# Two-layer block on one core: another order of product, squares, silu, low parts and fourth powers in the first stage

## The chip, the core and the metric

The kernel runs on one NeuronCore of a Trainium2 chip. It is one launch that holds the whole network: TensorE for the matrix products, VectorE, ScalarE and GpSimd beside it, SyncE for the loads and stores. The metric is the device time in microseconds. Lower is better.

## The reference

The input is 2048 tokens of width 256 (8 x 256 x 256, float32). Four parts follow each other, each with a residual sum and a layer norm:

```python
x = _layernorm(x + _L0_attn_ref(x, ...))   # 16 heads of 16, rope, layernorm of q and k, causal scores ** 4
x = _layernorm(x + _L0_ffn_ref(x, ...))    # silu(x @ gate.T) * (x @ up.T), hidden width 1024, then down
x = _layernorm(x + _L1_attn_ref(x, ...))   # 32 heads of 8, softmax with a relative bias
x = _layernorm(x + _L1_ffn_ref(x, ...))    # 8 experts, top 2, and a shared expert
```

The change lies in the first two of these. Of the first attention, for each batch of 256 tokens:

```python
q = layernorm(rope(q), ln_scale, ln_bias)
k = layernorm(rope(k), ln_scale, ln_bias)
a = tril(einsum(q, k) ** 4)
out = einsum(a / sum(a), v)
```

## The kernel before

Every float32 product is made of three matrix products of a high and a low part (`product3`, lines 443 to 445), so what enters a product is first written as a high part by ScalarE (`..._hi`) and then, as the difference to it, a low part by VectorE (`..._lo`).

The first stage takes the first attention and the first feed-forward net together. It has 8 iterations `i` of one batch of 256 tokens, and each has 8 slots `p`, one for each pair of heads. All engines run a program of their own, in an order that is written out by hand in the functions `slot` and `narrow_slot` (and in `dense` for what fills a slot), and they wait for each other at semaphores alone. An engine works strictly in the order in which its program stands: a wait holds back all that is written behind it.

What a slot holds, by engine, with the lines that a profile shows:

- TensorE: `scores` of pair p (729, 730), `gate_up(m)` of one hidden tile of 128 of the feed-forward net of an earlier batch (12 products `ps<-WU` of 128x256), in odd slots `mix` (747, the product with v of four heads), then a part of the attention of this or the next batch (`heads`, 676, turns q and k; `v`; `qk`; `x_turn`; `c_turn`; `ct_turn`, 697; `project`), and last `down(m - 1)` (6 products `ps<-WU`).
- ScalarE: `square` of the scores (1398), `hidden_hi(m - 1)` (1417), in even slots `quartic` of the odd pair p - 1 (1381), `silu(m)` (1410), and others, among them `centred_squares(i + 1)` (1352), `deviation(i + 1)` (1357), `head_hi_parts(i + 1)` (1368) and `x_hi` (1309).
- VectorE: in odd slots `quartic` of the even pair p - 1 (1937), `hidden_lo(m - 1)` (1955), `product(m)` (1949, up part times silu), and the chain that makes q and k of the next batch: `rope_half` (1881 to 1884), `rotated` (1889 adds, 1890 sums over each head), `centre` (1895), `variance` (1900), `normalised` (1907, 1908), `times_scale` (1914), `plus_bias` (1918), `lo_parts` (1928). Further `x1_added` and `x1_statistics` (1825 to 1833) and `x1_norm` (1841), the norm behind the feed-forward net, `context_lo` (1804) and `x_lo` (1776).
- GpSimd: `masks` (2511), the lower triangle of each squared pair; in iteration 2 also the low parts of the weights (2463).

Iterations 0 and 1 have no feed-forward tiles yet and run `narrow_slot`; iterations 2 to 7 run `slot`. The feed-forward net lags by `LAG1 = 2` batches, so m = 8 * (i - 2) + p - 1. After iteration 7 stand 16 more tiles of it, and then the second attention and the experts, which the change does not touch.

The waits that tie the engines in a slot:

```python
pe.wait_ge(prod_ready[1], m)              # gate_up(m): the bank of gates must be read by product(m - 1)
pe.wait_ge(hid_ready[1], m + 1)           # down(m): hidden_lo(m)
pe.wait_ge(ffn_step, 3 * b - 2)           # down(m) of a batch's first tile: x1_added of the batch before
act.wait_ge(quartic_even, H0 // 4 * i + p // 2)   # square(i, p), even p: quartic(i, p - 2)
act.wait_ge(in_step, IN_STEPS * b + 8)    # centred_squares(b): centre(b)
act.wait_ge(in_step, IN_STEPS * b + 13)   # head_hi_parts(b): plus_bias(b)
dve.wait_ge(hid_hi[1], m + 1)             # hidden_lo(m): hidden_hi(m)
dve.wait_ge(masked, H0 // 2 * i + p + 1)  # quartic(i, p): masks(i, p)
pe.wait_ge(ct_ready[0], i)                # project and heads of the next batch: context_lo(i - 1)
```

Of the kernel before, what the change touches and what calls it, by code (L numbers as in the profile page):

```python
# [47 lines left out]
LAG1 = 2  # L48
# [39 lines left out]
def program(nc, x, rope, ln, aw0, wu1, aw2, rel, wu3, router, sel, out):  # L88
    with ExitStack() as ctx:
# [1213 lines left out]
        def _(act):  # L1303
# [37 lines left out]
            def first_layer():  # L1341
# [6 lines left out]
                n = iterations[0]  # L1348

                def centred_squares(b):  # L1350
                    act.wait_ge(in_step, IN_STEPS * b + 8)
                    act.square(SQ, CEN).then_inc(cen_squared, 1)
# [52 lines left out]
                def silu(m):  # L1405

                    act.wait_ge(gate_ready[1], m + 1)
                    if m >= 2:
                        act.wait_ge(prod_ready[1], m - 1)
                    act.activation(sg[:, m % 2, :], ps[:, gate_bank(m), 0:S], ACT.Silu).then_inc(silu_ready[1], 1)  # L1410
# [74 lines left out]
                def slot(i, p):  # L1485

                    m = H0 // 2 * (i - LAG1) + p - 1
                    square(i, p)
                    if p == 2 and i < n - 1:
                        centred_squares(i + 1)  # L1490
                    if m >= 1:
                        hidden_hi(m - 1)
                    if p % 2 == 0 and (p or i):
                        quartic(i, p - 1, not i)
                    if m >= 0:
                        silu(m)
                    dense(i, p)
                    if i == LAG1 and p < TILES1 - 1:
                        raw_hi(p + 1)
                    if p == 3 and i < n - 1:  # L1500
                        deviation(i + 1)
# [232 lines left out]
        def _(dve):  # L1734
# [109 lines left out]
            def first_layer():  # L1844
# [22 lines left out]
                n = iterations[0]  # L1867
# [18 lines left out]
                def rotated(b):  # L1886

                    dve.wait_ge(in_step, IN_STEPS * b + 6)
                    step(rope_added, b + 1, dve.tensor_tensor(ROT, ROT, ROT2, ALU.add))
                    step(in_step, IN_STEPS * b + 7, dve.tensor_reduce(hsum, rh, AX_X, ALU.add))  # L1890

                def centre(b):
# [64 lines left out]

                def narrow_slot(i, p):

                    if p % 2:  # L1960
                        quartic(i, p - 1, not i)
                    if p == 1:
                        rotated(i + 1)
                    if p == 2:
                        centre(i + 1)
                    if p == 3:
                        times_scale(i + 1)
                        if i:
                            for c in range(2):
                                context(0, i - 1, c, D0)  # L1970
                        variance(i + 1)
                    if p == 4:
                        x_lo(0, i + 2)
                        normalised(i + 1)
                    if p == 5:
                        if i:
                            context_lo(0, i - 1)
                        plus_bias(i + 1)
                    if p == 6:
                        lo_parts(i + 1, 0)  # L1980
                        lo_parts(i + 1, 1)
                        if i:
                            dve.wait_ge(y_ready[0], i)
                            add(0, i - 1, 2, xr_a, (B_Y[0],))
                            statistics(0, i - 1, 2, xr_a)
                    if p == 7:
                        if i:
                            norm(0, i - 1, 2, xr_a, X1[(i - 1) % 2])
                        dve.wait_ge(split_ready[0], 8 * (i + 2))
                        rope_half(i + 2, 0)  # L1990
                        if not i:
                            rope_half(i + 2, 1)

                def slot(i, p):

                    m = H0 // 2 * (i - LAG1) + p - 1
                    left = n - 1 - i
                    if p % 2:
                        quartic(i, p - 1, not i)
                    if m >= 1:  # L2000
                        hidden_lo(m - 1)
                    if p == 1 and left:
                        rotated(i + 1)
                    if p == 2 and i > LAG1:
# [13 lines left out]
                    if p == 0:  # L2018
                        x1_lo(i - LAG1)
                        if left:  # L2020
                            rope_half(i + 1, 1)
                    if p == 1 and left:
                        centre(i + 1)
                    if p == 2 and left:
                        variance(i + 1)
# [6 lines left out]
                    if p == 4:  # L2032
                        if left:
                            plus_bias(i + 1)
                        if i > LAG1:
                            x1_norm(i - LAG1 - 1)
                    if p == 5 and i:
                        context_lo(0, i - 1)
                    if p == 5 and left:
                        lo_parts(i + 1, 0)  # L2040
                    if p == 6 and i:
                        dve.wait_ge(y_ready[0], i)
                        add(0, i - 1, 2, xr_a, (B_Y[0],))
                        statistics(0, i - 1, 2, xr_a)
# [7 lines left out]
                diagonal()  # L2052
                rope_half(0, 1)
                rotated(0)
                centre(0)
                times_scale(0)
                variance(0)
# [680 lines left out]
```

## Time and profile before

| | |
|---|---|
| device time, median of 3 runs | 912.49 us (912.26 to 913.99) |
| the profiled execution | 913.56 us, its span 911.8 us |
| mean granted clock of TensorE | 0.974 of full speed |
| busy in the span | PE 90%, PEld 76%, DVE 72%, ACT 64%, POOL 48% |
| iterations 0 and 1 | about 30 to 80.5 us from the span's start |
| iteration 2 | about 80.5 to 124 us |
| iterations 3 to 7 | about 124 to 316 us, 39.1 us each, the last 35.4 us |

In a profile PE is TensorE, DVE VectorE, ACT ScalarE, POOL GpSimd. In a row of the timeline the first number is the start, the second the time taken, both in us; the bracket gives how long the engine stood idle before it and which engine and line released it. Consecutive matmuls overlap, so their times sum to more than the clock shows. A row that joins several instructions says xN.

### The profile page before, as it was taken

The numbers are of one execution on the slowest core, as the hardware profiler recorded it, in microseconds if no ns is written. First come the engines' busy times: TensorE is split into PE (matmuls) and PEld (weight loads), VectorE is DVE, ScalarE is ACT, GpSimd is POOL, SyncE is SP. The second block draws the span as 40 slices with busy tenths as digits, with TensorE's granted clock in tenths as the row PEclk, the third lists the DMA queues.
The fourth block names the chain that finished last, engine by engine and source line by source line (L and its number), as shares of the span: only waits on it lengthen the run. The fifth ranks groups of instructions, "written<-read, shape, count | busy, mean of one in ns | idle before, by whom it ended". The sixth has DMA issues, their size and how long they took to land.

```text
span 911.8 us, 20877 instructions
## 1 busy us (share of the span) xinstructions
PE 819.4 (90%) x7136; PEld 692.3 (76%) x7136; DVE 653.8 (72%) x2050; ACT 581.4 (64%) x1230; POOL 435.2 (48%) x733
## 2 busy tenths in 40 slices
PE   3877889999989999789999999999988999899994
PEld 2555778888878899666777777776766888899984
DVE  6978779788885555778798888889785553365447
ACT  2787958677685533678777777778765233366646
POOL 0346632332343220566766767666754366244423
PEclk9899999999999999899999999999999899899998
DMA  7201220210000010101020221101013112244434
GB/s 209 69 3 46 72 82 13 82 47 1 25 24 25 25 47 12 52 22 29 22 61 14 60 59 27 52 22 41 22 56 122 40 65 82 82 123 120 127 140 184
DMA packets 54761, 54.86 MB, mean 60 GB/s; under 512 B 17953, under 2 KB 48929, under 8 KB 54658
## 3 DMA queue, kind: packets, MB, share of 16 engines
q1 hardware_dynamic: 51250, 44.18, 16.7%
q0 software_dynamic: 3408, 9.34, 2.9%
q8 instruction: 60, 0.98, 0.4%
q14 instruction: 43, 0.35, 0.1%
HBM read 32.85 MB, written 20.65 MB: 59 GB/s over the span
## 4 chain that ended last, share of the span: by engine, by line
PE 60%; DVE 14%; ACT 11%; issue 7%; POOL 5%; DMA 3%; SPq 0%; ACTq 0%; DVEq 0%; POOLq 0%
PE ps L443 11%; PE ps L978 10%; PE ps L445 10%; PE ps L444 10%; PE ps L992 7%; POOL xs L2630 3%; ACT G L1566 2%; PE ps L963 2%; PE ps L676 2%; ACT G L1564 2%; PE ps L747 2%; PE ps L689 1%; DVE G L2127 1%; DVE ring L1937 1%; PE ps L1192 1%
## 5 line engine op out<-in xcount | busy, mean ns | idle before, releaser
L2511 POOL TENSOR_SCALAR_AFFINE_SELECT G<-G 128x256 f32<-128x256 f32 x128 | 77.2, 626 | 145.1 <-ACT G L1398 144.9
L1564 ACT ACTIVATE G<-ps 128x512 f32<-128x512 f32 x184 | 102.8, 602 | 49.8 <-PE ps L978 49.8
L443 PE MATMUL ps<-WU 128*128 128x256 f32 x384 | 117.1, 305 | 17.1 <-DVE wu_rows L1949 6.9
L2566 POOL TENSOR_SCALAR G<-G,small 128x256 f32<-128x256 f32 x214 | 99.4, 480 | 55.2 <-DVE small L2127 54.4
L2127 DVE CUSTOM_DVE_ANT_0 G<-ps,nb 128x256 f32<-128x256 f32 x296 | 108.3, 420 | 10.6 <-PE ps L963 9.7
L444 PE MATMUL ps<-WU 128*128 128x256 f32 x384 | 108.6, 283 | 0.0
L445 PE MATMUL ps<-WU 128*128 128x256 f32 x384 | 108.6, 283 | 0.0
L443 PEld LDWEIGHTS ps<-WU 128*128 128x128 f32 x384 | 73.0, 190 | 25.5 <-issue 9.3
L2566 POOL TENSOR_SCALAR wu_rows<-wu_rows,small 128x256 f32<-128x256 f32 x154 | 71.5, 479 | 42.9 <-DVE small L2127 42.6
L978 PE MATMUL ps<-ident,G 128*128 128x128 f32 x592 | 85.3, 282 | 4.2 <-ACT G L1564 4.2
L2127 DVE CUSTOM_DVE_ANT_0 wu_rows<-ps,nb 128x256 f32<-128x256 f32 x216 | 79.5, 420 | 7.9 <-PE ps L963 6.1
L978 PEld LDWEIGHTS ps<-ident,G 128*128 128x128 f32 x592 | 65.3, 143 | 15.6 <-issue 6.2
L1398 ACT ACTIVATE G<-ps 128x768 f32<-128x768 f32 x64 | 52.3, 817 | 37.0 <-PE ps L730 33.1
L444 PEld LDWEIGHTS ps<-WU 128*128 128x128 f32 x384 | 73.4, 191 | 0.4
L445 PEld LDWEIGHTS ps<-WU 128*128 128x128 f32 x384 | 73.3, 191 | 0.0
L992 PE MATMUL ps<-G 128*18 128x256 f32 x1024 | 61.5, 380 | 11.7 <-ACT G L1566 8.8
L2669 POOL DMA_INDIRECT yy<-G x39 | 37.4, 959 | 59.9 <-ACT G L1665 59.9
L978 PE MATMUL ps<-ident,wu_rows 128*128 128x128 f32 x432 | 61.7, 278 | 2.9 <-ACT G L1564 2.9
L992 PEld LDWEIGHTS ps<-G 128*18 128x18 f32 x1024 | 30.7, 97 | 34.3 <-issue 14.7
L978 PEld LDWEIGHTS ps<-ident,wu_rows 128*128 128x128 f32 x432 | 46.8, 140 | 10.9 <-issue 4.5
L443 PE MATMUL ps<-AW,RT 128*128 128x512 f32 (+1 forms) x128 | 48.5, 379 | 5.2 <-DVE AW L1849 3.9
L1410 ACT ACTIVATE wu_rows<-ps 128x256 f32<-128x256 f32 x64 | 24.3, 379 | 43.8 <-PE ps L445 43.7
(260 smaller groups left out, 2402.6 us busy)
## 6 DMA issues: line engine op xcount, KB each, us to landing
xs<-G SPq DMA_DIRECT2D x8, 645.0 KB, 6.6
G<-xs SPq DMA_DIRECT2D x39, 128.0 KB, 2.2
G<-x SPq DMA_DIRECT2D x17, 256.0 KB, 3.0
G<-in_x SPq DMA_DIRECT2D x16, 256.0 KB, 2.9
wu_rows<-yy SPq DMA_DIRECT2D x8, 512.0 KB, 7.2
x<-G SPq DMA_DIRECT2D x15, 256.0 KB, 2.2
wu_rows<-in_wu SPq DMA_DIRECT2D x8, 384.0 KB, 5.8
wraw<-in_wu SPq DMA_DIRECT2D x8, 256.0 KB, 2.7
```

The lines of the kernel that those rows point to most:

```text
L443: pe.matmul(o, lh, rh, start=start, stop=False, skip_group_check=True)
L444: pe.matmul(o, lh, rl, start=False, stop=False, skip_group_check=True)
L445: return pe.matmul(o, ll, rh, start=False, stop=stop, skip_group_check=True)
L978: m = pe.transpose(ps[:, 2 + n % 2, S * kt + P * t:S * kt + P * (t + 1)], prob(n)[:, t, P * kt:P * (kt + 1)], ident[:])
L992: m = pe.matmul(ps[32 * j:32 * j + TWO, SHARED_BANK, 0:S], vp2[:, kt, at:at + TWO], probT(h)[:, kt, :], start=half == 0 and kt == 0, stop= ...
L1398: act.square(U(p), ps[:, b:b + 2, 0:384]).then_inc(squared, 1)
L1564: act.activation(probT(n), halves(2 + n % 2), ACT.Exp).then_inc(probT_taken, 1)
L2127: m = dve.tensor_tensor_reduce(prob(n)[:, t, :], ps[:, SCORE_BANKS[n % 4], S * t:S * (t + 1)], nbv[:, t, :], 1.0, -FMIN, ALU.add, ALU.min, ...
L2511: m = pool.affine_select(out=u, in_=u, compare_op=ALU.is_ge, fill=0.0, base=0, pattern=[[0, 2], [1, P]], channel_multiplier=-1)
L2566: m = pool.tensor_scalar(p, p, -1.0, mneg[:, k:k + 1], ALU.mult, ALU.add)
L2630: pool.indirect_dma_start(xs, bass.IndirectOffsetOnAxis(ap=at, axis=0), X[:, b, :], None).then_inc(block_moved[g], 16)
L2669: pool.indirect_dma_start(yy, bass.IndirectOffsetOnAxis(ap=at, axis=0), yo[i % 3], None).then_inc(y_sent[i % 3], 16)
```

## The change

No instruction is added or taken out; the program of TensorE and that of SyncE are the same word for word. On ScalarE, in `slot`, `centred_squares` moves from directly behind `square` to behind `silu` (slot 2), and in slot 4 `quartic` moves behind `silu`. On VectorE, in `slot`, the sums over the heads become a function of their own, `head_sums`, that stands behind `product` instead of ahead of it (slot 1); `hidden_lo` comes ahead of `quartic` in slot 5; and `x1_norm` moves from the end of slot 4 to the end of slot 5. In `narrow_slot` the quartic of pair 4 moves from the start of slot 5 to the start of slot 4.

```diff
@@ ScalarE, slot(i, p)
                     square(i, p)
-                    if p == 2 and i < n - 1:
-                        centred_squares(i + 1)
                     if m >= 1:
                         hidden_hi(m - 1)
-                    if p % 2 == 0 and (p or i):
+                    if p % 2 == 0 and p != 4 and (p or i):
                         quartic(i, p - 1, not i)
                     if m >= 0:
                         silu(m)
+                    if p == 4:
+                        quartic(i, p - 1, not i)
+                    if p == 2 and i < n - 1:
+                        centred_squares(i + 1)
                     dense(i, p)
@@ VectorE, rotated(b)
                     step(rope_added, b + 1, dve.tensor_tensor(ROT, ROT, ROT2, ALU.add))
+
+                def head_sums(b):
+
                     step(in_step, IN_STEPS * b + 7, dve.tensor_reduce(hsum, rh, AX_X, ALU.add))
@@ VectorE, narrow_slot(i, p)
-                    if p % 2:
+                    if p % 2 and p != 5:
                         quartic(i, p - 1, not i)
                     if p == 1:
                         rotated(i + 1)
+                        head_sums(i + 1)
...
                     if p == 4:
+                        quartic(i, p, not i)
                         x_lo(0, i + 2)
                         normalised(i + 1)
@@ VectorE, slot(i, p)
-                    if p % 2:
+                    if p % 2 and p != 5:
                         quartic(i, p - 1, not i)
                     if m >= 1:
                         hidden_lo(m - 1)
+                    if p == 5:
+                        quartic(i, p - 1, not i)
...
                     if p == 1 and left:
+                        head_sums(i + 1)
                         centre(i + 1)
...
                     if p == 4:
                         if left:
                             plus_bias(i + 1)
-                        if i > LAG1:
-                            x1_norm(i - LAG1 - 1)
...
                     if p == 5 and left:
                         lo_parts(i + 1, 0)
+                    if p == 5 and i > LAG1:
+                        x1_norm(i - LAG1 - 1)
```

The order of the instructions as it comes out, at three places. The line numbers of VectorE move by 2 to 5 with the change (1937 becomes 1942, 1949 becomes 1954, 1955 becomes 1960). First VectorE in slots 4 and 5 of iteration 0, a narrow one; `ring<-G` is `quartic`, `RT<-ps,RT` is `x_lo`. Before:

```order
L1900 TENSOR_REDUCE small<-G 128x64
L1776 TENSOR_TENSOR RT<-ps,RT 128x512
L1907 RECIPROCAL small<-small 128x64
L1908 TENSOR_TENSOR G<-G,small 128x1024
L1937 TENSOR_TENSOR ring<-G 128x768
L1918 TENSOR_TENSOR G<-G,lnt 128x1024
```

And now:

```order
L1905 TENSOR_REDUCE small<-G 128x64
L1942 TENSOR_TENSOR ring<-G 128x768
L1778 TENSOR_TENSOR RT<-ps,RT 128x512
L1912 RECIPROCAL small<-small 128x64
L1913 TENSOR_TENSOR G<-G,small 128x1024
L1923 TENSOR_TENSOR G<-G,lnt 128x1024
```

The quartic of pair 4 has moved ahead of three instructions, and `plus_bias` (1918, now 1923) follows `normalised` at once. Second, ScalarE in slots 2 and 4 of iteration 3 as differences; `WU<-wu_rows` is `hidden_hi`, `ring<-G` `quartic`, `wu_rows<-ps` `silu`, and 1352 `centred_squares`:

```order
 L1398 ACTIVATE G<-ps 128x768
+L1417 CAST WU<-wu_rows 128x256
+L1381 ACTIVATE ring<-G 128x768
+L1410 ACTIVATE wu_rows<-ps 128x256
 L1352 ACTIVATE G<-G 128x1024
-L1417 CAST WU<-wu_rows 128x256
-L1381 ACTIVATE ring<-G 128x768
-L1410 ACTIVATE wu_rows<-ps 128x256
 L1386 COPY G<-ps 128x512
```

```order
 L1398 ACTIVATE G<-ps 128x768
 L1417 CAST WU<-wu_rows 128x256
-L1381 ACTIVATE ring<-G 128x768
 L1410 ACT_TABLE_LOAD
 L1410 ACTIVATE wu_rows<-ps 128x256
+L1381 ACTIVATE ring<-G 128x768
 L1313 CAST RT<-ps 128x512
```

In slot 2 the squares have gone behind three instructions; in slot 4 the load of the activation table and `silu` come ahead of the quartic. Third, VectorE of iteration 3 from the end of slot 4 through slot 5 up to the first instruction of slot 6. Before:

```order
L1918 TENSOR_TENSOR G<-G,lnt 128x1024
L1841 TENSOR_SCALAR G<-G,small 128x256 x2
L1937 TENSOR_TENSOR ring<-G 128x768
L1955 TENSOR_TENSOR WU<-wu_rows,WU 128x256
L1776 TENSOR_TENSOR RT<-ps,RT 128x512
L1949 TENSOR_TENSOR wu_rows<-ps,wu_rows 128x256
L1804 TENSOR_TENSOR WU<-ps,WU 128x512
L1928 TENSOR_TENSOR RT<-G,RT 128x2x8x16 x4
L1955 TENSOR_TENSOR WU<-wu_rows,WU 128x256
```

And now:

```order
L1923 TENSOR_TENSOR G<-G,lnt 128x1024
L1960 TENSOR_TENSOR WU<-wu_rows,WU 128x256
L1942 TENSOR_TENSOR ring<-G 128x768
L1778 TENSOR_TENSOR RT<-ps,RT 128x512
L1954 TENSOR_TENSOR wu_rows<-ps,wu_rows 128x256
L1806 TENSOR_TENSOR WU<-ps,WU 128x512
L1933 TENSOR_TENSOR RT<-G,RT 128x2x8x16 x4
L1843 TENSOR_SCALAR G<-G,small 128x256 x2
L1960 TENSOR_TENSOR WU<-wu_rows,WU 128x256
```

`hidden_lo` (1955, now 1960) stands directly behind `plus_bias`, and `x1_norm` (1841, now 1843) has gone behind the first four low parts. In slot 1 of the same engine `product` now stands ahead of the reduce of 1890 in the same way.

## Rows read from the trace of the kernel before

**Rows 1.** Page, part 1: busy time of each engine, share, instructions.

```profile
PE 819.4 (90%) x7136; PEld 692.3 (76%) x7136; DVE 653.8 (72%) x2050; ACT 581.4 (64%) x1230; POOL 435.2 (48%) x733
```

**Rows 2.** Windows: length, busy PE, PEld, DVE, ACT, POOL, granted clock, DMA.

```profile
163.10:202.20 39.10, 37.38 (x330) 32.68 (x328) 32.95 (x64) 28.32 (x55) 11.77 (x20) 1.00 0.18 56
48.90:52.30 3.40, 3.37 (x17) 2.62 (x17) 3.33 (x8) 2.51 (x6) 1.76 (x2) 0.56 0.00 0
```

**Rows 3.** Timeline of TensorE, iteration 4: every row with idle ahead.

```profile
173.05 0.35 PE L443 MATMUL ps<-WU 128*128 128x256 f32 x1 [0.39 <-DVE wu_rows L1949]
...
176.70 0.35 PE L443 MATMUL ps<-WU 128*128 128x256 f32 x1 [0.54 <-DVE G L1825]
...
178.19 0.36 PE L443 MATMUL ps<-WU 128*128 128x256 f32 x1 [0.16 <-DVE wu_rows L1949]
...
187.02 0.36 PE L443 MATMUL ps<-WU 128*128 128x256 f32 x1 [0.24 <-DVE wu_rows L1949]
...
190.44 0.39 PE L443 MATMUL ps<-WU 128*128 128x256 f32 x1 [0.38 <-DVE WU L1955]
```

**Rows 4.** Timeline of VectorE, iteration 4, slots 1 to 6.

```profile
169.77 1.42 DVE L1889 TENSOR_TENSOR G<-G 128x1024 f32<-128x1024 f32 x1
171.22 1.22 DVE L1890 TENSOR_REDUCE small<-G 128x64 f32<-128x1024 f32 x1
172.48 0.42 DVE L1949 TENSOR_TENSOR wu_rows<-ps,wu_rows 128x256 f32<-128x256 f32 x1
...
175.52 0.43 DVE L1955 TENSOR_TENSOR WU<-wu_rows,WU 128x256 fp32r<-128x256 f32 x1 [1.49 <-ACT WU L1417]
...
177.96 1.21 DVE L1900 TENSOR_REDUCE small<-G 128x64 f32<-128x1024 f32 x1
...
186.44 0.42 DVE L1949 TENSOR_TENSOR wu_rows<-ps,wu_rows 128x256 f32<-128x256 f32 x1 [0.24 <-DVE G L1914]
...
188.04 0.74 DVE L1841 TENSOR_SCALAR G<-G,small 128x256 f32<-128x256 f32 x2
...
189.77 0.62 DVE L1955 TENSOR_TENSOR WU<-wu_rows,WU 128x256 fp32r<-128x256 f32 x1
...
194.17 0.43 DVE L1955 TENSOR_TENSOR WU<-wu_rows,WU 128x256 fp32r<-128x256 f32 x1 [0.91 <-ACT WU L1417]
```

**Rows 5.** Timeline of ScalarE, iteration 4, slots 2 and 4.

```profile
174.07 1.06 ACT L1352 ACTIVATE G<-G 128x1024 f32<-128x1024 f32 x1 [0.55 <-DVE G L1895]
175.03 0.39 ACT L1417 CAST WU<-wu_rows 128x256 fp32r<-128x256 f32 x1
...
184.68 1.28 ACT L1410 ACT_TABLE_LOAD   x1
185.97 0.38 ACT L1410 ACTIVATE wu_rows<-ps 128x256 f32<-128x256 f32 x1
```

**Rows 6.** Timeline of ScalarE, squares of pair 6, iterations 0 and 1.

```profile
45.09 0.81 ACT L1398 ACTIVATE G<-ps 128x768 f32<-128x768 f32 x1 [2.24 <-DVE ring L1937]
...
71.08 0.81 ACT L1398 ACTIVATE G<-ps 128x768 f32<-128x768 f32 x1 [1.52 <-DVE ring L1937]
```

**Rows 7.** Timeline of VectorE, iteration 1, slots 4 and 5.

```profile
67.45 0.69 DVE L1776 TENSOR_TENSOR RT<-ps,RT 128x512 fp32r<-128x512 f32 x1 [1.22 <-ACT RT L1309]
...
69.94 1.04 DVE L1937 TENSOR_TENSOR ring<-G 128x768 f32<-128x768 f32 x1
70.91 0.68 DVE L1804 TENSOR_TENSOR WU<-ps,WU 128x512 fp32r<-128x512 f32 x1
```

**Rows 8.** Timeline of TensorE, iterations 0, 1, 2 and 6.

```profile
48.90 3.36 PE L676 MATMUL ps<-ident,RT 128*128 128x128 f32 x16 [1.27 <-DVE RT L1928]
...
71.73 0.35 PE L443 MATMUL ps<-AW,WU 128*128 128x256 f32 x1 [2.90 <-DVE WU L1804]
...
93.29 0.39 PE L443 MATMUL ps<-WU 128*128 128x256 f32 x1 [0.67 <-DVE WU L1955]
...
269.38 0.38 PE L443 MATMUL ps<-WU 128*128 128x256 f32 x1 [1.21 <-DVE WU L1955]
```

More of the change, by code:

```diff
@@ L2054, in first_layer @@
                 rotated(0)
+                head_sums(0)
                 centre(0)
```

## The prediction

> **What bounds the kernel now.** I read the page first: TensorE is busy for 90% of the span, every other engine for 72% or less [rows 1]. Then busy time by window: in iteration 4 TensorE works 37.38 of 39.10 us at the full clock [rows 2]. So time can only come from TensorE's own idle time, or from stretches at the lower clock. Next the timeline of TensorE, for every row with idle time ahead of it. In iteration 4 there are five, 0.39, 0.54, 0.16, 0.24 and 0.38 us, together 1.71, and each was released by VectorE [rows 3]: three by `product` (1949), one by `x1_added` (1825), one by `hidden_lo` (1955). Iterations 3 and 5 repeat the first four within 0.02; iteration 3 has the fifth too, 5 lacks it. Iteration 6 repeats the first three; its two in slots 4 and 5 are 0.67 and 1.21, the second being in [rows 8], while GpSimd splits weights beside VectorE.
>
> Then what made VectorE late. In slot 1 it runs the add (1.42), the reduce (1.22) and only then `product`, at 172.48, though that product waits for nothing: no idle stands before it [rows 4]. TensorE's `gate_up` starts behind that product, at 173.05 [rows 3]. In slot 2 `hidden_lo` starts at 175.52 after 1.49 idle, waiting for ScalarE's 1417 [rows 4]; ScalarE had first waited 0.55 for `centre` and then run 1.06 of squares, so that 1417 started at 175.03 [rows 5]. `x1_added` stands behind this `hidden_lo`, and TensorE's `down` waits for it until 176.70 [rows 3]. In slot 4 `silu` comes behind the quartic and the table load, at 185.97 [rows 5], and `product` at 186.44 [rows 4]. In slot 5 `hidden_lo` comes at 189.77, behind `x1_norm` (188.04, 0.74) and a quartic [rows 4].
>
> In the narrow iterations 0 and 1, ScalarE's square of pair 6 waits 2.24 and 1.52 us for VectorE's quartic of pair 4 [rows 6]; behind it on ScalarE stand its own quartic, on which `mix` waits, and the high parts of the next heads. TensorE then idles 1.27 before `heads` in iteration 0, and 2.90 before `project` in iteration 1, which waits for `context_lo` [rows 8].
>
> **The change, part by part.** Nothing is added, so each part is the wait that it takes off TensorE, less what comes late in its place.
>
> *Slots 1 to 3, iterations 3 to 6.* `product` moves ahead of the 1.22 reduce: it starts near 171.25, ends by 171.6, and the 0.39 is gone. The reduce and `centre` end where they did, near 174.05. ScalarE no longer waits for `centre`: hidden_hi starts after the square, near 173.45 in place of 175.03, so that `hidden_lo` starts right behind `centre` at 174.05 and `x1_added` ends near 175.1. TensorE reaches `down` some 0.93 earlier, near 175.7; the 0.54 is gone too. `silu` waits for `gate_up` until about 174.4, and VectorE comes to `product` behind the statistics near 176.2 in place of 177.65, which takes off the 0.16. The squares now start near 174.8, 0.75 later than 174.07, and end near 175.85; `variance`, which needs them, stood at 177.96 [rows 4], so it is not late: it comes near 176.55. What is queued behind the squares on ScalarE is `outputs` and `place_v`; they end near 176.85, before the next scores. Sum 1.09 in each of four iterations: 4.4 us. This costs nothing only as long as the squares end before 177.96.
>
> *Slot 4, iterations 3 to 6.* The table load starts after hidden_hi and `silu` starts 0.85 earlier, near 185.15. `product` is then bound by `times_scale`, which ends near 186.2, and the 0.24 goes (0.67 becomes about 0.45 in iteration 6). ScalarE's quartic comes 1.7 later, near 186.4; its reader is the `mix` of slot 5, near 188.3. No cost.
>
> [...] By the row the table load takes 1.28, and `silu` starts 0.01 after it [rows 5]. [...]
>
> *Slot 5, iterations 2 to 6.* `hidden_lo` now waits only for hidden_hi, near 188.8, about 1 us earlier than 189.77, and the 0.38 (1.21 in iteration 6) goes. VectorE gives the 0.74 of `x1_norm` away here, but the quartic starts 0.5 later, so that the `product` of slot 5 ends as before, near 191.3. TensorE now wants it near 191.1. So of the 0.62 that slots 4 and 5 free, about 0.2 comes back as a wait in slot 6: 0.4 net in iterations 3 and 4, 0.2 in 5 (of 0.24), and 1.0 in 6 (of 1.43, since VectorE's next `product` stands in a chain that moves only 0.2). Sum 2.0. `x1_norm` falls into the 0.91 that VectorE idles before the `hidden_lo` at 194.17 [rows 4]; 0.74 fits. SyncE's store of x2 waits for it and starts 5 us later, ahead of the reload of the residual rows, which waits for a norm in slot 7 anyway. No cost.
>
> *Iteration 2.* It has no `x1_added`; its wait before `down` in slot 2 is 0.67 [rows 8], for the same `hidden_lo` behind the same squares. It goes: 0.7. The rest of its idle time waits for GpSimd's weight splits and for a product in slot 6, neither of which is touched.
>
> *Narrow iterations.* In iteration 1 VectorE sits idle 1.22 before `x_lo` [rows 7], and the quartic needs 1.04; its masks are then long done. So it costs nothing there, and `context_lo`, `plus_bias` and all high and low parts of the next heads move up by 1.0, with `project`, which waited 2.90 for `context_lo`. In iteration 0 the idle time is shorter, `x_lo` is 0.25 late, and 0.75 to 1.05 is won on `plus_bias` and on the start of the head parts: that is the 1.27 wait in [rows 8]. Sum 1.0 + 1.05 = 2.05.
>
> [...]
>
> **Sum**: 4.4 + 2.0 + 0.7 + 2.05 + 0.4 = 9.55 us. From the profiled 913.56 that is 904.0. The median of the runs lies 1.07 below the profiled execution; I forecast 903.0.
>
> **Rivals.**
>
> A. *The waits come back.* VectorE's chain in slots 4 to 7 is dense, and a `product` that moves no earlier catches TensorE each time. If slots 4 to 6 return nothing and the narrow part half, the sum is 4.4 + 0.7 + 1.0 = 6.1: 906.5. If also only the first of the three waits of slots 1 to 3 goes (4 x 0.39 = 1.6), it is 3.3: 909. For it: 0.2 of 0.62 already comes back in my own account. Against it: the three waits have more than 0.3 of margin each.
>
> B. *Nothing to be seen.* The gaps before `gate_up` are not VectorE's lateness but the handover itself, and reappear with any order. For it: they are small, 0.16 to 0.54. Against it: other `gate_up`s of the same iteration have no idle at all. Time: 912.5, within 1.8.
>
> C. *Slower.* The squares now wait for `silu`, and with them the whole chain to the next heads. It costs nothing until they end at 177.96 against the 175.85 that I expect; from there each us costs one in each of four iterations. At 4.5 us late it is 4 x 2.4 = 9.6, which eats the whole gain; at 5 it is 914 to 915. Only a `gate_up` that ended that late could do this, and it would need a wait that no row shows.
>
> [...]
>
> **How the numbers follow.** Forecast, between 901 and 905.5: 0.55. A: 0.22. B: 0.09. C: 0.05. D, or a gain over 11 us: 0.09. The range from 899.5 to 907.5 takes in D, the forecast and the near half of A: about 0.8. A change is told from none at about 0.2%, 1.8 us. Faster: forecast, D and nearly all of A, 0.86. Same 0.09, slower 0.05.
>
> **What would show it.** Right, if in iteration 4 of the changed kernel TensorE has no row with idle before the `gate_up` of slots 2 and 3 and `down` of slot 2, if 1417 of slot 2 directly follows 1398 on ScalarE, if the iterations 3 to 5 last 37.6 to 37.9 us, and if the square of pair 6 in iterations 0 and 1 no longer waits for VectorE. The table load of slot 4 should stand at 1.28 with `silu` right behind it. Wrong, if a new wait of over 0.3 us for `product` stands in slot 6 or 0, if `heads` waits for low parts in slots 6 and 7, if the narrow `x_lo` starts over 0.5 late behind a mask, or if the low clock shows up at a new place.

## The result and the profile after

The changed kernel takes 904.38 us (median of 14 runs), the kernel before, beside it, 913.35 us (14 runs): a ratio of 0.9906, 95% interval 0.9894 to 0.9919, or 8.6 us less (7.4 to 9.7). The ratio is that of the means, 904.50 and 913.06. The ratios below leave out four executions of e1, e2 and e4 and one of the kernel before that took 949 to 1543 us. The forecast was 903.0 against 912.49, a ratio of 0.9896, with a range down to 899.5 and up to 907.5. The profiled executions have spans of 901.9 and 911.8 us.

Page of the changed kernel, its first lines:

```profile
span 901.9 us, 20883 instructions
PE 815.6 (90%) x7136; PEld 689.3 (76%) x7136; DVE 653.4 (72%) x2050; ACT 580.9 (64%) x1230; POOL 436.1 (48%) x733
```

All busy times stay within 4 us of [rows 1]: nothing was made cheaper, only idle time went. Busy by window, one window of about an iteration (iteration 4, the columns as in [rows 2]):

```profile
161.10:198.70 37.60, 37.01 (x332) 32.60 (x328) 32.60 (x64) 28.17 (x55) 11.48 (x20) 1.00 0.18 57
```

37.01 of 37.60 us busy on TensorE, in place of 37.38 of 39.10 [rows 2]. Timeline of TensorE, iterations 0, 1, 2, 4 and 6, rows with idle ahead of them:

```profile
48.71 3.65 PE L676 MATMUL ps<-ident,RT 128*128 128x128 f32 x16 [1.62 <-DVE RT L1933]
...
70.42 0.36 PE L443 MATMUL ps<-AW,WU 128*128 128x256 f32 x1 [1.95 <-DVE WU L1806]
...
102.82 0.39 PE L443 MATMUL ps<-WU 128*128 128x256 f32 x1 [1.65 <-POOL WU L2474]
...
187.87 0.36 PE L443 MATMUL ps<-WU 128*128 128x256 f32 x1 [0.55 <-DVE wu_rows L1954]
...
258.19 0.36 PE L443 MATMUL ps<-WU 128*128 128x256 f32 x1 [0.47 <-DVE wu_rows L1954]
267.79 0.36 PE L443 MATMUL ps<-WU 128*128 128x256 f32 x1 [0.43 <-DVE wu_rows L1954]
272.59 0.36 PE L443 MATMUL ps<-WU 128*128 128x256 f32 x1 [0.23 <-DVE wu_rows L1954]
```

The five waits of [rows 3] are gone. One new one stands in iteration 4, 0.55 us before the `gate_up` of slot 6, and likewise in 3 and 5. The 0.67 of iteration 2 and the 1.21 of iteration 6 [rows 8] are gone. Timeline of VectorE in iteration 4, against [rows 4]:

```profile
168.85 0.42 DVE L1954 TENSOR_TENSOR wu_rows<-ps,wu_rows 128x256 f32<-128x256 f32 x1
169.20 1.21 DVE L1895 TENSOR_REDUCE small<-G 128x64 f32<-128x1024 f32 x1
...
171.70 0.51 DVE L1960 TENSOR_TENSOR WU<-wu_rows,WU 128x256 fp32r<-128x256 f32 x1
...
174.21 1.21 DVE L1905 TENSOR_REDUCE small<-G 128x64 f32<-128x1024 f32 x1
...
185.50 0.42 DVE L1960 TENSOR_TENSOR WU<-wu_rows,WU 128x256 fp32r<-128x256 f32 x1 [1.44 <-ACT WU L1417]
185.84 0.95 DVE L1942 TENSOR_TENSOR ring<-G 128x768 f32<-128x768 f32 x1
186.71 0.69 DVE L1778 TENSOR_TENSOR RT<-ps,RT 128x512 fp32r<-128x512 f32 x1
187.31 0.41 DVE L1954 TENSOR_TENSOR wu_rows<-ps,wu_rows 128x256 f32<-128x256 f32 x1
```

`product` now stands ahead of the reduce, and the `hidden_lo` of slot 2 follows `centre` with no idle, where it had waited 1.49. The last four rows are the new wait: `hidden_lo`, quartic, `x_lo` and only then the `product` that TensorE wants at 187.33, when its scores end; it ends at 187.72. Timeline of ScalarE in iteration 4, slots 2 and 4, against [rows 5]:

```profile
171.04 0.40 ACT L1417 CAST WU<-wu_rows 128x256 fp32r<-128x256 f32 x1
...
172.35 1.06 ACT L1352 ACTIVATE G<-G 128x1024 f32<-128x1024 f32 x1
...
179.76 0.40 ACT L1417 CAST WU<-wu_rows 128x256 fp32r<-128x256 f32 x1
180.18 1.28 ACT L1410 ACT_TABLE_LOAD   x1
181.48 0.38 ACT L1410 ACTIVATE wu_rows<-ps 128x256 f32<-128x256 f32 x1
184.61 0.43 ACT L1417 CAST WU<-wu_rows 128x256 fp32r<-128x256 f32 x1
```

The squares stand 1.3 us behind `hidden_hi` now. The table load starts 0.02 after `hidden_hi` ends and takes 1.28, and `silu` starts 0.02 behind it. In the kernel before, `silu` started 0.01 behind a load of 1.28 [rows 5].

To compare kernels below I take the time from one `x1_turn` (line 791, once in each iteration from 2 on) to the next, and for iterations 0 and 1 together from the first `heads` to the first `x1_turn`. This leaves out the start before and the other stages behind, which vary from one execution to the next: from the last `x1_turn` to the end it is 576.5 in the kernel before, 574.3 after, and 574.3 to 579.1 in the experiments, none of which touches that part.

| us | 0 and 1 | 2 | 3 | 4 | 5 | 6 | 7 |
|---|---|---|---|---|---|---|---|
| before | 53.44 | 44.95 | 39.17 | 39.14 | 38.98 | 38.56 | 32.34 |
| after | 51.21 | 45.52 | 37.49 | 37.64 | 37.48 | 36.29 | 32.34 |
| e1 slots 1 and 2 alone | 54.39 | 45.57 | 37.77 | 37.76 | 37.77 | 37.16 | 32.34 |
| e2 squares alone | 53.83 | 45.55 | 38.17 | 38.18 | 38.17 | 37.57 | 32.35 |
| e3 slots 4 and 5 alone | 54.64 | 45.03 | 38.87 | 38.86 | 38.84 | 37.64 | 32.35 |
| e4 narrow part alone | 51.13 | 44.88 | 39.15 | 39.14 | 39.15 | 38.56 | 32.33 |
| e5 after, product first in slot 5 | 51.12 | 45.60 | 37.39 | 37.60 | 37.39 | 36.27 | 32.36 |
| e6 after, masks of slot 5 held | 51.17 | 45.53 | 37.38 | 37.63 | 37.39 | 36.27 | 32.34 |
| e7 after, squares 1 us later | 51.12 | 44.03 | 37.48 | 37.62 | 37.50 | 36.28 | 32.35 |
| e8 after, x1_norm back | 51.24 | 45.54 | 37.42 | 37.41 | 37.41 | 36.28 | 32.34 |
| e9 e5 and e8 together | 52.19 | 44.84 | 37.41 | 37.40 | 37.39 | 36.30 | 32.34 |
| e10 e9, product first in slot 6 too | 51.19 | 45.40 | 36.94 | 36.91 | 36.94 | 36.77 | 32.35 |
| e11 after, squares in slot 3 | 52.27 | 47.51 | 41.14 | 41.14 | 41.10 | 39.57 | 32.35 |

Two things in the table do not come from the edits. Iteration 5 of the kernel before is 0.17 shorter than that of e4, whose program is the same there. And the first two columns carry the clock, which differs from one execution to the next (6.8 us at a granted 0.50 in e4, 20.5 in e1): with the old order of the narrow part the first one reads 53.44 to 54.64, with the new one 51.12 to 52.27.

Summed over these and the 21.2 up to the next `x1_turn` the stage goes from 307.79 to 299.17: 8.62 us, the same as the ratio of the runs gives.

### The profile page after: what moved, and what is told of

The parts are those of the page before. It is cut to its first block, busy times and chain, and to the rows that moved or that the text cites. A ratio compares the mean times of both kernels' runs of the same rounds, so it can differ in the third digit from the quotient of the medians.

```text
span 901.9 us, 20883 instructions
## 1 busy us (share of the span) xinstructions
PE 815.6 (90%) x7136; PEld 689.3 (76%) x7136; DVE 653.4 (72%) x2050; ACT 580.9 (64%) x1230; POOL 436.1 (48%) x733
## 4 chain that ended last, share of the span: by engine, by line
PE 69%; DVE 11%; ACT 11%; issue 5%; POOL 2%; DMA 1%; another core or an unknown queue 0%; DVEq 0%; ACTq 0%; SPq 0%; POOLq 0%
PE ps L443 13%; PE ps L444 12%; PE ps L445 12%; PE ps L978 10%; PE ps L992 7%; ACT G L1568 2%; PE ps L963 2%; PE ps L676 2%; ACT G L1566 2%; PE ps L747 2%; PE ps L689 1%; DVE G L2138 1%; PE ps L729 1%; PE ps L948 1%; PE ps L1215 1%
```

## The experiments

### The four parts, each alone

**e1, slots 1 and 2 alone**, on the kernel before:

```diff
-                    if p == 2 and i < n - 1:
-                        centred_squares(i + 1)
                     if m >= 1:
                         hidden_hi(m - 1)
...
                         silu(m)
+                    if p == 2 and i < n - 1:
+                        centred_squares(i + 1)
@@ VectorE
                     if p == 1 and left:
+                        head_sums(i + 1)
                         centre(i + 1)
```

> The parts of slots 1 and 2 alone on the kernel before: squares behind silu, product ahead of the head sums. My theory, that each wait is worth what its row says: TensorE loses the three waits of slots 1 to 3 (1.09 us) in iterations 3 to 6 and the 0.67 of iteration 2, while the 0.24 and 0.38 of slots 4 and 5 stay: 5.1 us less, ratio 0.9944. Rival A, the waits come back later in the iteration: iterations 3 to 5 last 38.5 us or more and the gain is under 3 us. Rival B, handover: no gain, the same idle in front of gate_up.

Measured: 0.9929 (0.9905 to 0.9953), 6.5 us. Timeline of TensorE, iteration 4, all rows with idle ahead:

```profile
186.66 0.36 PE L443 MATMUL ps<-WU 128*128 128x256 f32 x1 [0.24 <-DVE wu_rows L1952]
190.08 0.39 PE L443 MATMUL ps<-WU 128*128 128x256 f32 x1 [0.38 <-DVE WU L1958]
```

The first three waits of [rows 3] are gone, the last two stand as they were, to the hundredth. So the waits are independent, and neither A nor B holds. But the iteration is 1.38 us shorter, where the three waits sum to 1.09. In the whole stage the profile of e1 is 3.8 us shorter and not 6.5, since its iterations 0 to 2 are 1.6 longer than before; they hold more of the low clock, 20.5 us at a granted 0.50 against 13.7.

**e2, the squares alone** (the ScalarE half of e1's edit).

> The move of the squares behind silu alone, product still behind the head sums. My theory: the 0.54 before down and the 0.16 of slot 3 go (0.7 in four iterations, 0.67 in iteration 2), the 0.39 before the gate_up of slot 2 stays: 3.5 us less, ratio 0.9962, iterations 3 to 5 at 38.4 us. Rival C, late squares cost: the new start of the squares behind silu delays variance, and iterations get longer than 39.1.

Measured: 0.996 (0.9944 to 0.9975), 3.7 us. Timeline of TensorE, iteration 4:

```profile
173.51 0.35 PE L443 MATMUL ps<-WU 128*128 128x256 f32 x1 [0.39 <-DVE wu_rows L1949]
...
186.51 0.35 PE L443 MATMUL ps<-WU 128*128 128x256 f32 x1 [0.24 <-DVE wu_rows L1949]
189.94 0.39 PE L443 MATMUL ps<-WU 128*128 128x256 f32 x1 [0.40 <-DVE WU L1955]
```

The 0.54 and the 0.16 belong to the squares, the 0.39 to the product behind the reduce. The iteration lost 0.96 for waits of 0.70.

**e3, slots 4 and 5 alone**, on the kernel before:

```diff
-                    if p % 2 == 0 and (p or i):
+                    if p % 2 == 0 and p != 4 and (p or i):
                         quartic(i, p - 1, not i)
...
                         silu(m)
+                    if p == 4:
+                        quartic(i, p - 1, not i)
@@ VectorE
                         hidden_lo(m - 1)
+                    if p == 5:
+                        quartic(i, p - 1, not i)
...
-                        if i > LAG1:
-                            x1_norm(i - LAG1 - 1)
...
+                    if p == 5 and i > LAG1:
+                        x1_norm(i - LAG1 - 1)
```

> The parts of slots 4 and 5 alone: silu ahead of the quartic, hidden_lo ahead of the quartic, x1_norm a slot later. My theory, corrected by the trace after: 0.24 and 0.38 go and 0.5 comes back before the gate_up of slot 6, so 0.1 in iterations 3 to 5 and 1.0 in 6: about 1.3 us less in all, ratio 0.9986, hardly to be told from none. Rival: these slots carry the gain: 2 us or more, no wait in slot 6.

Measured: 0.9995 (0.9982 to 1.0009), which can't be told from none. The table can: 0.30, 0.28, 0.14 and 0.92 in iterations 3 to 6, 1.64 us (with e4's iteration 5 for the one before, the 0.14 is 0.31). Timeline of TensorE, iteration 4:

```profile
174.99 0.36 PE L443 MATMUL ps<-WU 128*128 128x256 f32 x1 [0.39 <-DVE wu_rows L1951]
...
178.64 0.36 PE L443 MATMUL ps<-WU 128*128 128x256 f32 x1 [0.55 <-DVE G L1827]
...
180.13 0.36 PE L443 MATMUL ps<-WU 128*128 128x256 f32 x1 [0.17 <-DVE wu_rows L1951]
...
193.41 0.36 PE L443 MATMUL ps<-WU 128*128 128x256 f32 x1 [0.54 <-DVE wu_rows L1951]
```

The 0.24 and the 0.38 have become one wait of 0.54 before slot 6.

**e4, the narrow part alone**, on the kernel before (`quartic(i, p, not i)` in slot 4 in place of slot 5).

> The earlier fourth power of pair 4 in iterations 0 and 1 alone. My theory: ScalarE no longer waits for VectorE there, heads of iteration 1 and project come 1.0 to 1.2 us earlier each: 2.1 us less, up to 3 where the low clock around them goes: ratio 0.9977 to 0.9967. Rival: what is won is lost before iteration 2, since VectorE's chain through the norm to x1_turn decides there: under 1 us.

Measured: 0.997 (0.9955 to 0.9984), 2.7 us, and 2.31 in the table. Timeline of TensorE, iterations 0 and 1:

```profile
47.44 1.06 PE L676 MATMUL ps<-ident,RT 128*128 128x128 f32 x8 [1.62 <-DVE RT L1928]
48.82 1.15 PE L676 MATMUL ps<-ident,RT 128*128 128x128 f32 x8 [0.32 <-ACT RT L1313]
50.81 0.50 PE L443 MATMUL ps<-AW,RT 128*128 128x512 f32 x1 [0.85 <-DVE G L1884]
...
69.12 0.36 PE L443 MATMUL ps<-AW,WU 128*128 128x256 f32 x1 [1.96 <-DVE WU L1804]
```

Counted from the first `heads` (27.51 before, 28.48 after, 27.25 here), this `heads` comes at 21.39 before, 20.23 after and 20.19 here, and `project` at 44.22, 41.94 and 41.87. So each narrow iteration wins 1.1 to 1.2. The other kernels bear this out. Each of the four with the old order has `heads` at 21.39 to 21.45, each of the nine with the new one at 20.17 to 20.37. From the `mix` of iteration 1 that waits 1.5 to `project` it is 15.48 in all four and 14.52 to 14.54 in the nine, but for e9 (15.44), where a stretch of low clock (0.50 for 3.4 us) lies in between. Most of what is left of the spread in the table lies between that `heads` and that `mix`: 7.1 to 7.4 us, and 7.7 to 8.3 in e1, e2, e3 and e11, where the granted clock is 0.50 for 6.8 us there. Here the transposes run at the full clock (1.00 from 47.44 to 49.97), 1.06 and 1.15 for eight, where the changed kernel took 3.65 for sixteen, at a mean of 0.53; and `project` comes no earlier for it, since TensorE then waits 0.85 for the rope.

The parts add up. In iterations 3 to 6 e1 wins 5.39 us and e3 1.64, together 7.03; the whole change wins 6.95. The ratios of e1, e3 and e4 multiply to 0.9894, that of the whole is 0.9906 (0.9894 to 0.9919), which agrees but says less, since the interval of e1 alone is 0.0048 wide.

### The new wait before slot 6

**e5**, the changed kernel with `product(m)` directly behind `hidden_lo(m - 1)` in slot 5, ahead of the quartic:

```diff
                     if p == 5:
+                        product(m)
                         quartic(i, p - 1, not i)
...
-                    if m >= 0:
+                    if m >= 0 and p != 5:
                         product(m)
```

> The changed kernel with product directly behind hidden_lo in slot 5, ahead of the quartic and x_lo. My theory: the new wait of 0.55 before the gate_up of slot 6 is this product standing behind a quartic (0.95) and x_lo (0.69); ahead of them it is 1.5 us earlier and the wait goes in iterations 3 to 6: 2.1 us below the changed kernel, iterations 3 to 5 at 37.0 us, ratio to before 0.9883. Rival: the wait moves on once more, to heads or to product in slot 6 (x_lo, context_lo and low parts are 0.4 later), and the iterations stay at 37.5.

Measured: 0.9887 (0.9868 to 0.9906), and iterations of 37.39, 37.60, 37.39. The rival was right. Timeline of TensorE, iteration 4:

```profile
194.06 0.36 PE L443 MATMUL ps<-WU 128*128 128x256 f32 x1 [0.51 <-DVE wu_rows L1954]
```

The wait before slot 6 is gone, and this one stands before slot 7, for the `product` behind the low parts of slot 6.

**e6**, the changed kernel with the masks of pair 5 held back on GpSimd until `hidden_lo` has ended:

```diff
                 pool.wait_ge(squared, H0 // 2 * i + p + 1)
+                if p == 5 and i >= LAG1:
+                    pool.wait_ge(hid_ready[1], H0 // 2 * (i - LAG1) + p - 1)
```

> The changed kernel with one more wait on GpSimd: the masks of pair 5 start only when the hidden_lo of slot 5 has ended. [...]

Measured: 0.9886 (0.9864 to 0.9909). Timeline of VectorE, iteration 4, and below it of GpSimd:

```profile
184.94 0.42 DVE L1960 TENSOR_TENSOR WU<-wu_rows,WU 128x256 fp32r<-128x256 f32 x1 [1.45 <-ACT WU L1417]
185.28 0.95 DVE L1942 TENSOR_TENSOR ring<-G 128x768 f32<-128x768 f32 x1
```

```profile
185.50 1.36 POOL L2524 TENSOR_SCALAR_AFFINE_SELECT G<-G 128x256 f32<-128x256 f32 x2 [4.67 <-DVE WU L1960]
```

In the changed kernel the masks start 0.68 ahead of `hidden_lo`, and I took them for what holds it back in iteration 4. Here they start 0.56 behind its start, and it is no earlier: 22.80 us after `x1_turn` in both kernels, although ScalarE's 1417 ends at 22.34. So the masks aren't what holds it. What they do cost is the quartic: in iterations 3 and 5 it takes 1.16 in the changed kernel and 0.95 here, and the wait before slot 6 falls from 0.54 to 0.34; in iteration 4 it took 0.95 in both, and the wait is 0.55 and 0.54. In iteration 3 of the changed kernel the mask had 0.35 us left when the quartic began, in iteration 4 it had ended 0.25 before. So 0.35 us beside a mask went with 0.21 more on the quartic. The held masks pay for it in turn: the first of them now starts while the quartic runs and takes 1.00 in iteration 4, where it takes 0.41 in the changed kernel.

**e8**, the changed kernel with `x1_norm` back at the end of slot 4:

```diff
                             plus_bias(i + 1)
+                        if i > LAG1:
+                            x1_norm(i - LAG1 - 1)
...
-                    if p == 5 and i > LAG1:
-                        x1_norm(i - LAG1 - 1)
```

> The changed kernel with x1_norm back at the end of slot 4. My theory, from the trace after: in iterations 3 to 5 VectorE idles 1.44 before hidden_lo in slot 5, so 0.74 of x1_norm fits there and nothing changes; in iteration 6, where plus_bias is slowed beside GpSimd, hidden_lo gets 0.4 to 0.7 later: under 0.7 us in all, no difference that can be told. Rival: the move of x1_norm carries the gain of slot 5, and without it 0.4 comes back in each of iterations 3 to 6, 1.6 us or more.

Measured: 0.9877 (0.9856 to 0.9898). Timeline of VectorE, iteration 4:

```profile
184.91 0.73 DVE L1843 TENSOR_SCALAR G<-G,small 128x256 f32<-128x256 f32 x2
185.90 0.43 DVE L1960 TENSOR_TENSOR WU<-wu_rows,WU 128x256 fp32r<-128x256 f32 x1 [0.26 <-ACT WU L1417]
186.25 1.15 DVE L1942 TENSOR_TENSOR ring<-G 128x768 f32<-128x768 f32 x1
```

The norm fits in the idle time, as my theory said; its move was worth nothing. In iteration 4 it did harm: `hidden_lo` starts 0.03 behind the end of 1417 here and 0.46 behind it with the norm moved, and the iteration lasts 37.41, not 37.64. In iteration 6 it comes 0.93 later than in the changed kernel and makes `down` wait 0.18, but the iteration is no longer (36.28). It is not `plus_bias` that is slow there: beside GpSimd's 2463 that took 2.36 in the kernel before, but 1.22 here and 1.21 in the changed kernel. It is the norm, which takes 1.59 beside GpSimd's 2474, for 0.73 in iteration 4.

**e9**, e5 and e8 together.

> The changed kernel with x1_norm back in slot 4 and product ahead of the quartic in slot 5. My theory: with the product moved the wait before the gate_up of slot 6 goes, but one of 0.43 came up before the gate_up of slot 7, for the product that stands behind the low parts of slot 6; x1_norm isn't what holds that one, ScalarE's 1417 is, so it stays near 0.4 and iterations 3 to 5 last 37.3 to 37.4 us. Rival: x1_norm in slot 5 is what makes slot 6 late; without it there the wait falls under 0.1 and the iterations last 37.0.

Measured: 0.9891 (0.9873 to 0.9909), iterations of 37.40 and a wait of 0.44 before slot 7, as my theory had it: `x1_norm` isn't what holds that product either.

**e10**, e9 with `product` of slot 6 ahead of the second low parts:

```diff
-                    if p == 6 and left:
-                        lo_parts(i + 1, 1)
...
                     if m >= 0 and p != 5:
                         product(m)
+                    if p == 6 and left:
+                        lo_parts(i + 1, 1)
```

> The same with the product of slot 6 also ahead of the second low parts. My theory: TensorE has no wait left in iterations 3 to 5, they last 36.9 to 37.0 us, 0.5 less than in the changed kernel, and 6 lasts 35.8 or less: 2.1 us below it, ratio to before near 0.985 to 0.988. Rival: the low parts, 0.4 later, now hold heads or the norm of slot 7, the wait moves on a third time and the iterations stay at 37.4.

Measured: 0.9887 (0.9869 to 0.9905). Busy by window, iteration 4:

```profile
161.25:198.16 36.91, 36.87 (x331) 32.56 (x329) 32.44 (x64) 28.10 (x56) 11.51 (x21) 1.00 0.19 60
```

TensorE is busy for 36.87 of 36.91 us: no wait is left, and the iterations last 36.94, 36.91 and 36.94. Iteration 6 got 0.48 longer (36.77 for 36.29), with a wait of 0.58 before slot 7, and the whole wins 1.3 us on iterations 3 to 6 against the changed kernel, where I had expected 2.1. The runs can't tell that: their interval overlaps the changed kernel's.

### The slower rival, in two doses

**e7**, the changed kernel with `centred_squares` behind the two copies of slot 2, 1 us later (`dense(i, p)` ahead of it).

> The changed kernel with the squares moved further back, behind the two copies of slot 2 on ScalarE (about 1.1 us later). It tests rival C, the slower case. My theory: squares end near 1 us later, still before the slack of about 2 us in the old order is used, but product in slot 2 stands ahead of variance and is not late; variance comes 0.8 later, and with it the quartic, hidden_lo and product of slot 3, whose reader is the gate_up of slot 4 a full slot later: no wait, ratio to before 0.990 to 0.992 like the changed kernel. Rival: each microsecond of late squares costs one in each iteration: 4 us slower than the changed kernel, 0.995.

Measured: 0.9897 (0.9877 to 0.9918); iterations 37.48, 37.62, 37.50. The squares start 10.63 us after `x1_turn` in place of 9.65, `variance` 11.75 in place of 11.51 (I had expected 0.8 later), and no iteration from 3 on is longer.

**e11**, the same in slot 3:

```diff
-                    if p == 2 and i < n - 1:
+                    if p == 3 and i < n - 1:
                         centred_squares(i + 1)
                     dense(i, p)
```

> The changed kernel with the squares a whole slot later, behind the silu of slot 3 on ScalarE; VectorE's variance stands in slot 2 as before and waits for them. Rival C of the prediction with a dose beyond its threshold. My theory: variance starts near 3.4 us later than in the changed kernel, past the slack of 2; VectorE's product of slot 3 behind it is 3.4 late and TensorE's gate_up of slot 4 waits 1.5 to 2 us in iterations 3 to 6: 38.9 to 39.6 us each, 6 to 9 us slower than the changed kernel, ratio to before 0.997 to 1.001. Rival, slack everywhere: under 2 us slower.

Measured: 1.0067 (1.005 to 1.0085), slower than both kernels. Timelines of VectorE and of TensorE, iteration 4:

```profile
183.85 1.22 DVE L1905 TENSOR_REDUCE small<-G 128x64 f32<-128x1024 f32 x1 [3.21 <-ACT G L1352]
...
185.85 0.42 DVE L1960 TENSOR_TENSOR WU<-wu_rows,WU 128x256 fp32r<-128x256 f32 x1
```

```profile
186.32 0.39 PE L443 MATMUL ps<-WU 128*128 128x256 f32 x1 [2.06 <-DVE WU L1960]
```

`variance` waits 3.21, and `hidden_lo` of slot 3 behind it makes TensorE wait 2.06 before `down`; my theory had it at the `gate_up` of slot 4, behind the product. Busy by window, before and behind that wait:

```profile
175.00:186.00 11.00, 9.26 (x85) 8.05 (x83) 7.51 (x14) 8.74 (x15) 2.92 (x6) 1.00 0.00 1
186.00:193.00 7.00, 6.68 (x44) 6.30 (x44) 6.83 (x12) 4.63 (x8) 1.59 (x2) 0.76 0.01 2
```

Behind the wait the granted clock falls to a mean of 0.76: it is 0.50 for 3.4 of the 7 us, and so in each of iterations 3 to 6. Against e10, matmul by matmul, the wait sets TensorE back by 2.3 us, the low clock by 1.5 more, and a wait of 0.43 before slot 7 by 0.5. That makes the iteration 3.5 us longer than the changed kernel's, where I had expected 1.5 to 2.

## Why the prediction was right, step by step

**Slots 1 to 3: the mechanism right, the size too small.** The term was 1.09 in each of four iterations, 4.4; e1 measures 1.40, 1.38, 1.21 and 1.40, 5.4. I had priced a wait at the idle time of its row. That time counts from the end of the matmul ahead, as the profile models it; but without a wait the next matmul starts before that end. Timeline of TensorE in e10, which has no wait in iteration 4, at the `down` of slot 5:

```profile
184.00 0.66 PE L697 MATMUL ps<-ident,G 128*128 128x128 f32 x4
184.41 0.36 PE L443 MATMUL ps<-WU 128*128 128x256 f32 x1
```

The transposes end at 184.66 and `down` starts at 184.41, an overlap of 0.25. So a wait of 0.38 there costs about 0.63. At the `down` of slot 2 the overlap is 0.24, at the `gate_up` of slots 2, 3, 4 and 6 it is 0.07, 0.00, -0.04 and 0.07. For the three waits of slots 1 to 3, idle time and overlap sum to 1.09 + 0.31 = 1.40, as measured. For a whole iteration 4, from the 36.91 of e10: before, 36.91 + 1.71 + 0.52 = 39.14, measured 39.14; e1, 36.91 + 0.62 + 0.21 = 37.74, measured 37.76; e2, 36.91 + 1.03 + 0.28 = 38.22, measured 38.18; e3, 36.91 + 1.65 + 0.38 = 38.94, measured 38.86; after, 36.91 + 0.55 + 0.07 = 37.53, measured 37.64, where the `down` of slot 5 is late by 0.1 too and still overlaps, so that no row shows it.

**Slot 4: right.** `silu` came ahead of the table load's old place, the wait of 0.24 went, and the load took what its row said, 1.28.

**Slots 4 to 6: right in what comes back, too small in how much.** I put the returning wait at 0.2 and the sum of these slots at 2.0; e3 measures 1.64, and the wait is 0.54. VectorE did what I forecast: in e3 the `product` of slot 5 ends 26.26 us after `x1_turn`, and 26.25 before. TensorE is what I had wrong. Its scores of slot 6 end at 25.86 in e3 and at 26.73 before, 0.87 earlier, where I had taken off the 0.62 of the two rows; that is the mis-sized term of above once more, in slots 4 and 5. And `gate_up` starts 0.15 behind the end of `product`, which I had not counted. So the `product` is 0.40 late and the wait 0.55. In the changed kernel it is the same (scores 24.62, `product` 25.02, `gate_up` 25.17). Since e3 leaves slots 1 to 3 alone, the wait does not come from what they freed.

**x1_norm: right that it needs no time of its own, wrong that it had to be moved.** In e8, with the norm back, iterations 3 to 5 are even 0.07, 0.23 and 0.07 shorter than in the changed kernel; e9 says the same of slot 6.

**Iteration 2: the wait went, the gain did not come.** I had 0.7. The wait of 0.67 is gone from the trace, but the iteration got 0.57 longer. Behind the 1.65 wait for GpSimd, which the change does not touch, the granted clock falls to 0.50 for 3.4 us. Busy by window over that wait and the time behind it, the changed kernel:

```profile
98.90:106.20 7.30, 5.65 (x44) 4.55 (x46) 7.00 (x9) 5.44 (x10) 6.31 (x6) 0.81 0.00 0
```

And e7, the same place in the program:

```profile
96.80:104.10 7.30, 5.64 (x58) 4.86 (x56) 7.00 (x9) 5.72 (x11) 6.31 (x6) 1.00 0.01 2
```

e7 has the same wait and the full clock behind it, and its iteration 2 lasts 44.03: 0.92 less than before, as the wait of 0.67 and an overlap of 0.24 should give. So a fall of the clock takes 1.5 us back here. In the sum the clock stood at +0.4.

**Narrow iterations: right.** Expected 2.05, measured 2.2 (after) and 2.3 (e4). The wait before `heads` is longer than before, 1.62 for the 1.27 of [rows 8], and that reads like a failure until one counts from the start: it begins earlier, and its end is 1.16 earlier too. By the parts of e4 above, the order gives 1.16 and 0.96 of the 2.2; the other 0.1 to 0.2 can be the clock, which is at 0.50 for 10.2 us in these two iterations before and for 3.4 after.

**The clock term: the sign was luck.** The 0.4 in the sum was an estimate of mine, and no run shows it. I expected it at the transposes of iteration 0. They are as slow as before (3.65 at a mean clock of 0.53, for 3.36 at 0.56), and e4 shows that with the full clock (1.00) nothing is won there. The clock gave nothing at the transposes and took 1.5 in iteration 2.

**The sum.** 4.4 + 2.0 + 0.7 + 2.05 + 0.4 = 9.55 was forecast. Measured in the stage: 5.4 (slots 1 to 3) + 1.56 (after against e1 in iterations 3 to 6) - 0.57 + 2.23 = 8.62. Slots 1 to 3 were 1.0 too small, slots 4 to 6 and iteration 2 together 1.7 too large, and the narrow iterations with the clock term 0.2 too large. That the total came out within 1 us of the forecast is in part luck: terms that were 1.0 too small stood against terms that were 1.9 too large.

**The signs that I had named.** Those of being right came: the rows before the `gate_up` of slots 2 and 3 and the `down` of slot 2 are gone, 1417 follows 1398 at once in slot 2, the square of pair 6 no longer waits in iterations 0 and 1, and the table load is as it was. Only the iterations were a little off, 37.49, 37.64 and 37.48 for 37.6 to 37.9. But two of the signs of being wrong came as well: the wait for `product` in slot 6 is over 0.3, and the low clock stands at a new place, in iteration 2. The others did not: `x_lo` is 0.08 late in iteration 0, and in iterations 3 to 6 `heads` has no wait.

**The rivals.** A (the waits come back) is refuted for slots 1 to 3 by e1 and true in part for slots 4 to 6. B is refuted: the waits went with the order. C's threshold holds: I had put it at squares that end 12.89 us after `x1_turn` (177.96 less 165.07). They end at 10.71 in the changed kernel and at 11.72 in e7, which costs nothing, and at 14.77 in e11, which costs 3.5 us per iteration. Its price was too small: one us for each us past the threshold would be 1.9, and the low clock behind the wait (0.50 for 3.4 us) is most of the rest. A gain over 11 us, which was D, did not occur.

## What to carry to other kernels

Where one engine is busy for 95% of a stage, read every row of it that has idle time ahead, name for each what stands in front of the late instruction on the engine that released it, and move the ready one ahead of the one that can wait; the waits of different slots then came off one by one here and added up (5.39 and 1.64 us alone, 6.95 together). Each costs the idle time of its row and what the matmuls would overlap there without it, here 0.07 at most before a `gate_up` and 0.24 before a `down`. Follow the chain one slot further than the fix: each product that kept its place caught the faster engine again here, and it took the product moved in slot 5 and in slot 6 (e5, e10), with a wait of 0.5 between them in slot 7, to be rid of the last one in iterations 3 to 5. Compare such edits by the length of the iteration, not by the time of the program: e3 and e10 show 0.3 to 0.7 us in each of iterations 3 to 5, which repeat to within 0.03 where the program is the same (but for the 0.17 in the one iteration 5), and the runs could not tell either from its neighbour.

## What the runs showed of the hardware

- A wait of TensorE sets its stream back by the idle time of its row and by the overlap that the row has without a wait: 0.39 by 0.46 and 0.54 by 0.61 before a `gate_up`, 0.38 by 0.63, 0.54 by 0.77 and 2.06 by 2.31 before a `down` (before, e3, e11, each against e10).
- A wait of 1.65 us, for the same instruction of GpSimd, was followed by 3.4 us at a granted clock of 0.50 in the changed kernel, e1, e2, e5, e6, e8 and e10, and not in the kernel before, e3, e4, e7 and e9. The one cost 1.5 us against the other (45.52 and 44.03 for iteration 2). So seven of the nine kernels with the moved squares that have this wait show it and none of the three without, but e7 and e9 do without it. What decides is open.
- A wait of 2.06 us before `down` was followed by the low clock in all five iterations in which it stood (e11: 0.50 for 6.8 us in iteration 2, for 3.4 us in each of iterations 3 to 6), and the low clock cost 1.5 us in iteration 4 too.
- `hidden_lo` of slot 5 starts 0.46 us behind the end of ScalarE's instruction in iteration 4, and 0.10 to 0.11 behind it in iterations 3 and 5, in the changed kernel, e5, e6 and e7 alike, and 0.03 behind it in all three in e8, e9 and e10. In the first four VectorE has stood idle for 1.1 us or more by then, in the others for 0.25, but e3, with 1.1 in all three iterations, has 0.11 in all. The masks are not the cause (e6). What it is stays open.
